# GpSimd's order in the scan's ticks: the low part of a feed-forward chunk ahead of the norm's centring and scaling and of the step sizes

## The reference

```
x = layernorm(x + linear_attention(x))
x = layernorm(x + ffn0(x))        # silu(x W1) * (x W3), Hadamard transform, W2
x = layernorm(x + selective_scan(x))
x = layernorm(x + ffn1(x))        # silu(x Wg) * (x Wu), Wd

selective_scan(u):                # per token: 512 features, 32 states each
  rank, B, C = u W_bc             # 64, 32 and 32 columns
  delta = softplus(rank W_dt + b)
  h = exp(delta * A) * h + (delta * u) * B
  y = sum over states of h * C,  plus u * D_param
```

## Time and profile before

| what | value |
|---|---|
| three runs | 1846.28, 1846.84, 1851.75 us (median 1846.84) |
| the profiled execution's own time | 1851.74 us |
| its span, first to last instruction | 1850.0 us |
| TensorE busy | 1758.8 us (95%), mean granted clock 0.987 |
| VectorE busy | 1252.1 us (68%) |
| GpSimd busy | 1194.2 us (65%) |
| ScalarE busy | 1190.2 us (64%) |
| DMA | 427.29 MB, 68.3% of 16 engines' span |

### The profile page before, as it was taken

How to read it: one execution, slowest core, us unless ns; L and a number is a source line. 1 busy time by engine, 2 the same in 40 slices (tenths; PEclk the granted TensorE clock), 3 DMA queues, 4 the chain that set the end, 5 groups by cost and what they waited for, 6 DMA issues and landing times. The chain is left out here.

```text
span 1850.0 us, 26792 instructions
## 1 busy us (share of the span) xinstructions
PE 1758.8 (95%) x9472; PEld 1134.4 (61%) x9472; DVE 1252.1 (68%) x1336; ACT 1190.2 (64%) x1775; POOL 1194.2 (65%) x932
## 2 busy tenths in 40 slices
PE   7898989889989999999999999998999999999998
PEld 5666666566756556555555656554656566667886
DVE  2524252433119999789888999887999999993212
ACT  5453443498857777787767777676776767656443
POOL 4634345255617887789976997789987888772111
PEclk9999999999999999999999999999999999999999
DMA  7443323487938988789776997777878777865652
GB/s 250 133 127 96 125 76 131 134 284 249 324 121 288 314 306 274 232 287 325 242 243 214 329 318 255 243 246 263 279 262 296 249 263 273 290 237 166 210 193 91
DMA packets 159222, 427.29 MB, mean 231 GB/s; under 512 B 30992, under 2 KB 54096, under 8 KB 158704
## 3 DMA queue, kind: packets, MB, share of 16 engines
q1 hardware_dynamic: 159088, 425.57, 68.3%
HBM read 356.30 MB, written 69.21 MB: 230 GB/s over the span
## 5 line engine op out<-in xcount | busy, mean ns | idle before, releaser
L1837 POOL TENSOR_TENSOR q_or_raw_or_h_times_c<-h_states,c_rep 128x512 f32<-128x512 f32 x293 | 376.5, 1297 | 82.1 <-DVE h_states L1730 53.0
L1609 ACT ACTIVATE decay<-delta_on_states,a_neg 128x512 f32<-128x512 f32 x512 | 350.9, 716 | 23.9 <-DMA delta_on_states<-delta 22.3
L1715 DVE TENSOR_TENSOR du_spread_in_d_b<-du_spread_in_d_b,b_rep 128x1024 f32<-128x1024 f32 x256 | 310.9, 1215 | 56.1 <-PE du_spread_in_d_b L1434 55.6
L1730 DVE TENSOR_TENSOR_SCAN h_states<-decay,h_last,du_spread_in_d_b 128x512 f32<-128x512 f32 x256 | 318.4, 1270 | 7.1
L1837 POOL TENSOR_TENSOR h_times_c_rest<-h_states,c_rep 128x512 f32<-128x512 f32 x219 | 281.2, 1295 | 63.3 <-DVE h_states L1730 40.4
L1730 DVE TENSOR_TENSOR_SCAN h_states<-decay,du_spread_in_d_b 128x512 f32<-128x512 f32 x256 | 302.7, 1209 | 13.9 <-ACT h_last L1614 6.9
L1789 POOL TENSOR_TENSOR h_lo<-v_or_silu_in_h_lo,h_hi 128x512 fp32r<-128x512 f32 x128 | 166.1, 1298 | 177.0 <-ACT h_hi L1515 176.8
L111 PE MATMUL y_or_aux<-h_hi,w 128*128 128x512 f32 x468 | 223.0, 476 | 11.8 <-POOL h_lo L1789 10.5
L1434 PE MATMUL du_spread_in_d_b<-stack,selectors 96*128 96x512 bf16 x512 | 201.1, 393 | 0.3 <-DVE h_states L1730 0.3
L1680 DVE TENSOR_TENSOR v_or_silu_in_h_lo<-v_or_silu_in_h_lo,up_or_scores 128x512 f32<-128x512 f32 x128 | 86.6, 677 | 145.3 <-PE up_or_scores L113 126.6
L1515 ACT CAST h_hi<-v_or_silu_in_h_lo 128x512 fp32r<-128x512 f32 x128 | 78.9, 616 | 164.6 <-DVE v_or_silu_in_h_lo L1680 164.5
(11 more groups left out here) (235 smaller groups left out, 3862.0 us busy)
## 6 DMA issues: line engine op xcount, KB each, us to landing
delta_on_states<-delta SPq DMA_DIRECT2D x256, 512.0 KB, 5.6
w<-w_split SPq DMA_DIRECT2D x112, 512.0 KB, 5.6
attn_w_hi_or_x_hi_w<-w_split SPq DMA_DIRECT2D x112, 512.0 KB, 5.3
attn_w_lo_or_x_lo_w<-w_split SPq DMA_DIRECT2D x112, 512.0 KB, 5.2
w_split<-w_presplit_hi_lo SPq DMA_DIRECT2D x32, 512.0 KB, 3.5
w_presplit_hi_lo<-in_w13b SPq DMA_DIRECT2D x32, 256.0 KB, 3.6
w_split<-attn_w_hi_or_x_hi_w SPq DMA_DIRECT2D x8, 1024.0 KB, 6.9
w_split<-attn_w_lo_or_x_lo_w SPq DMA_DIRECT2D x8, 1024.0 KB, 6.8
```

The lines of the kernel that those rows point to most:

```text
L1609: act.activation(da[:, s % ND], dring[:, s % NR], ACT.Exp, scale=a[:, column(s):column(s) + 1]).then_inc(s_da, 1)
L1715: dve.tensor_tensor(both, both, brep[:, tile_of(s // SPO) % 2].unsqueeze(1).to_broadcast([P, 2, TT]), ALU.mult).then_inc(s_db, 1)
L1730: dve.tensor_tensor_scan(hs[:, s % NH], da[:, s % ND], uu[:, s % NU], initial, ALU.mult, ALU.add).then_inc(s_hs, 1)
L1837: pool.tensor_tensor(hc[s % NC_], hs[:, s % NH], crep[:, tile_of(s // SPO) % 2], ALU.mult).then_inc(s_hc, 1)
```

## The change

In GpSimd's loop, the call of `h_low` moves from behind the norm's `centre` and `scale` and the scan's `step_size` and `step_input` to the place in front of them, still behind `times_c`. No instruction is added or removed, and the other engines' programs stay as they are.

```diff
--- before.py
+++ after.py
@@ -1846,6 +1846,8 @@
                         part_low(0, 0)
                     if 0 <= s - 1 < STEPS:
                         times_c(s - 1)
+                    if tick in H_SPLIT_AT:
+                        h_low(H_SPLIT_AT[tick])
                     for e, k in CENTRE_AT.get(tick, ()):
                         if e in NORM_IN_SCAN:
                             centre(e, k)
@@ -1856,8 +1858,6 @@
                         step_size(*SIZE_AT[tick])
                     if tick in INPUT_AT and INPUT_AT[tick][0]:
                         step_input(*INPUT_AT[tick])
-                    if tick in H_SPLIT_AT:
-                        h_low(H_SPLIT_AT[tick])
                     if tick in SPLIT_AT:
                         x_low(*SPLIT_AT[tick])
                     if tick - 1 in W2_HIGH_AT:
```

## The result

The change makes the kernel 1.7 thousandths slower: median 1851.47 us over 20 runs against 1848.49 us over 20 runs of the kernel before on the same chips, ratio 1.0017 with a 95% interval of 1.0010 to 1.0025.

A forecast was written before the change was run, and what follows sets the result against it. TensorE, without a gap in the scan, was taken to set the end. Losses at chunks 34, 50, 83 and 99 less the gain at chunk 75 gave +2.97 us: 1849.8 us, range 1845.2 to 1853.4.

The forecast's parts named there:

- The rule of the five places: Chunks 34, 50, 66, 82, 98: GpSimd waits for the cast, not the inverse root; slips of 1.12 to 1.65 us.
- Chunk 75: Low part starts at 1276.96 instead of 1278.19, so TensorE's wait of 4.21 us shrinks to 2.98: gain 1.23 us.
- The eight places at nothing: Chunks 37, 39, 46, 54, 56, 70, 89, 91: taken as 0; bounds 0 and one further slip of 1.25 us.
- The sum: Chunks 34, 50, 66, 83, 99 and 75: 0.93 + 1.65 + 0 + 0.86 + 0.76 - 1.23 = +2.97 us.
- The absolute forecast: Whole kernel: 1846.84 + 3.0 = 1849.8 us against the median of the runs.
- the stretch of lower clock between 912 and 916: TensorE after the pause of 1.91 us at 911.5: granted clock 0.59, priced at 1.6 us.
- The second stretch: TensorE between 920 and 926: granted clock 0.50, the level of 1.2 GHz, priced at 3.0 us.
- the pause of 2.12 us at 347.98: TensorE's next matmul took 0.47 us, read as full clock and as evidence against a slower clock at chunk 50.
- the clock rival: Chunk 50: longer wait for norm 5's scales lowers TensorE's clock; +4.6 or +6.0 us in all; chance 0.22.
- Faster: Slips absorbed, and the shorter pause at chunk 75 no longer lowers the clock: -4.2 us, 1842.6; chance 0.05.
- no loss at all: Slips absorbed because GpSimd may be further ahead in unprofiled executions: -1.2 to +0.9 us, 1845.6 to 1847.7; chance 0.17.

The follow-up runs named there:

- The runs with the shifted cast: Changed kernel with ScalarE's cast at chunks 34, 50, 66, 82, 98 before its tick's decay (1.0001) or behind the next tick's (1.0038), against the kernel before.
- The exchange: Low part of chunk 75 put in front of norm 7's last centring; alone against the kernel before, 0.9984 and, run again, 0.9996.
- the late cast: Changed kernel with ScalarE's cast at chunks 34, 50, 66, 82, 98 behind the next tick's decay; against the kernel before 1.0038, 1856.08 us.
- the run on chunks 34, 50 and 66: Kernel before with the new `h_low` order at these three chunks only; 1.0019 (1.0008 to 1.0029), 1851.62 us.
- the run on chunks 82 and 98: Kernel before with the new `h_low` order at these two chunks only; 1.0010 (0.9999 to 1.0021), 1849.88 us.
- the run on the three `rank_of` places: Kernel before with the new `h_low` order at chunks 34, 50 and 66 only; 1.0019 (1.0008 to 1.0029), 1851.62 us.
- the run with the exchange alone: Kernel before with only chunk 75's low part in front of norm 7's last centring; 0.9984 (1846.23 us), run again 0.9996 (1847.6 us).

## Why the prediction came out as it did

**The rule of the five places held.** ScalarE's order root, decay, cast sets the slip: 1.12, 1.64, 1.12, 1.22 and 1.12 us measured against 1.12, 1.65, 1.12, 1.22 and 1.13. The hand-off of 0.08 us and the margins carried over into the new trace (but for that of chunk 66, larger than it needed to be): the losses were forecast as 0.93, 1.65, 0, 0.86 and 0.76 us and measured as 1.01, 1.57, 0.01, 0.81 and 0.76. The runs with the shifted cast show that the cast is the cause.

**Chunk 75.** The exchange shifts the low part by 1.2 us (11.4 to 11.5 us after the resumed gate matmul in six kernels with the old order, 10.2 to 10.3 in six with the exchange). The wait was forecast as 3.0 and is 2.9 to 3.0 in five of the six. In the sixth, with the late cast, it is 1.32: a half-speed stretch ahead of it turned part of the wait into work, and the low part comes at the same time.

I left the clock at this place as it was. That may be too little: from the resumed gate matmul to the spread matmul at about 1289 us (index 330, counted from 0) the six traces with the old order take 19.9 to 21.3 us, mean 20.8, and the six with the exchange 17.9 to 20.0, mean 18.9. The difference of 1.9 us is 0.7 more than the earlier low part gives. In four of the six traces with the old order the half-speed stretch at this place was twice as long as in the others; with the exchange that was so in one of six. With six traces each, and a spread of 1.4 to 2.1 us inside each group, this is a hint and no more.

**The eight places at nothing.** No run shows a loss there, but the time, 1.0005 (0.9996 to 1.0013), leaves room for one slip.

**The sum.** The forecast difference was 2.97 us; the medians differ by 2.98 us. With an interval of 1.8 to 4.6 us this closeness is luck; that the five places came in one by one is not. The profiled span was forecast as 1853.0 us and is 1851.5, because chunk 75 gave 0.85 us more and the rows of the balance that have nothing to do with the edit sum to -0.6 us. The absolute forecast, 1849.8, was 1.7 us too low, because it stood on a median of three runs (1846.84) that twenty runs put at 1848.49.

**The clock: one term was mis-sized, one row misread.** I priced the stretch of lower clock between 912 and 916 at 1.6 us. It costs nothing, because TensorE has a wait right behind it that ends with GpSimd. TensorE in the timeline of the run on chunks 34, 50 and 66, with no half-speed matmuls behind the pause:

```profile
912.44 0.62 PE L1443 MATMUL scan_y<-q_or_raw_or_h_times_c,sum_selectors 128*32 128x512 f32 x2 [1.89 <-POOL h_times_c_rest L1837]
...
921.08 0.50 PE L111 MATMUL y_or_aux<-h_hi,w 128*128 128x512 f32 x1 [4.12 <-POOL h_lo L1789]
```

And in that of the run on chunks 82 and 98, with half-speed matmuls:

```profile
911.11 1.00 PE L1443 MATMUL scan_y<-q_or_raw_or_h_times_c,sum_selectors 128*32 128x512 f32 x2 [1.89 <-POOL h_times_c_rest L1837]
...
919.74 0.50 PE L111 MATMUL y_or_aux<-h_hi,w 128*128 128x512 f32 x1 [2.52 <-POOL h_lo L1789]
```

From one resumption to the next it is 921.08 - 912.44 = 8.64 us and 919.74 - 911.11 = 8.63 us. The slow matmuls only turn 1.6 us of waiting into 1.6 us of work, and that is why the wait for low part 47 is 2.5 or 4.1 us in these traces. The second stretch, 920 to 926, stands behind that wait and does cost: the kernel before takes 2.8 us more from the pause at 911.5 to the fifteenth spread matmul than the six kernels that have the old place of low part 47 and no such stretch, near the 3.0 us of my price.

The misread row is the pause of 2.12 us at 347.98. I took the next matmul, 0.47 us, as proof that the clock held, and set it against the clock rival. But the fall only came later. Stretches of the kernel before, columns as in the earlier trace rows (with no work on GpSimd):

```profile
348.00:350.00 2.00, 2.00 (x8) 1.63 (x9) 1.64 (x3) 1.88 (x2) 0.00 (x0) 0.87 0.04 14
350.00:352.00 2.00, 2.00 (x7) 1.51 (x6) 0.00 (x0) 0.00 (x0) 0.00 (x0) 0.50 0.00 0
```

So in this trace both pauses were followed by half speed, and the argument against the clock rival was weaker than I wrote. It stayed away at chunk 50 in both traces all the same. The forecast did not hang on these terms, since the clock was taken as unchanged; the rivals did. "Faster" had the shorter pause at chunk 75 as its mechanism, and there a stretch at half speed does cost, since nothing waits right behind it. But one came behind the pauses of 2.91 to 3.02 us in all five traces as behind those of 4.1 to 4.3, so the shorter pause did not buy it off. The rival "no loss at all" is refuted by the mile posts and by the run on the three `rank_of` places (1.0008 at the least).

## What to carry to other kernels

When an operation is moved in front of another on an in-order engine, ask first when its input is there, and not how long it takes: here moving a subtraction of 1.25 us forward put its own length only on the operations that it overtook, but made everything behind it wait for a cast that the other engine makes after the result that the old order waited for. Then follow the slip to the next place where the critical engine asks, which may be one unit later, and subtract the margin that this place has. And move single places rather than whole rules: of 14 places here one gained, four lost and nine did nothing, and a place that the rule did not touch (chunk 47) gained more than the one that it helped.

## What the runs showed of the hardware that was not expected

The same pause does not always give the same clock. After the pause of 1.9 us near 911 us the granted clock fell to 0.50 within 6 us in ten of the fourteen traces and stayed at 1.00 up to the next wait in four; after the pause of 2.1 us near 348 us it fell within 2 us in three of the fourteen. So here the longer of two pauses was followed by half speed less often, and its length alone does not tell. After pauses of 2.9 to 3.0 us at chunk 75 the clock fell in all five traces, but the first matmul does not always show it: it took 0.79 or 0.80 us in three kernels and 0.50 us in two, where the clock fell about 1 us later (in the run with the exchange alone it is 0.50 from 1281 to 1283 us, after the matmul of 1279.09).

ScalarE's wait for a store moves with no edit. Near 1264 us it rounds a part of the step input, and cannot until the store of the part before has landed. In five kernels the store was in time and the wait ended with GpSimd; in nine the store ended it. The row in the run with the exchange at chunk 75 alone:

```profile
1264.42 0.62 ACT L1597 CAST delta_x_parts_out<-soft_in_x_hi 128x512 bf16<-128x512 f32 x1 [2.65 <-POOL soft_in_x_hi L1829]
```

And in the run with that low part in front of the product with C, whose program is the same up to there:

```profile
1264.81 0.62 ACT L1597 CAST delta_x_parts_out<-soft_in_x_hi 128x512 bf16<-128x512 f32 x1 [3.52 <-DMA delta_x_parts<-delta_x_parts_out]
```

The `silu` behind it tends to be late too: TensorE's wait for it is 0.5 to 1.4 us in the five traces (mean 0.9) and 0.9 to 2.4 in the nine (mean 1.9). The ranges overlap, and no run changed the store alone, so that the store makes the `silu` late is likely and not shown. If it does, it is one source of the several microseconds by which executions of one kernel differ.
